# FFN weight signs moved to the head of attention, one store awaited later, a fill split over two engines, bias loads moved: a conv + attention + FFN kernel on one Trainium2 core

## Chip, cores and metric

One core of one Trainium2 chip runs the whole program. The metric is the device time of one execution in microseconds (us). The kernel before takes 2920.16 us, the median of 3 runs (2918.62 to 2920.73).

## What is computed

The input `x` is 32 images of 96 channels and 32 x 32 positions. Three residual stages follow each other:

```python
x = x + _L0_conv_ref(_gn(x), ...)          # per image: linear attention over 1024 positions, plus an MLP
t = _to_tokens(x)                          # (32, 1024, 96)
t = t + _L1_attn_ref(_ln_t(t), ...)        # 6 heads of 16, causal softmax attention, 192 (image, head) pairs
t = t + _L1_ffn_ref(_ln_t(t), W1, b1, W2, b2)
```

The FFN uses weights that are reduced to their signs about a mean, in five groups of output features:

```python
for g in range(NUM_GROUPS):                # 5 groups; rows past 5 * gs stay zero
    wg = W[g * gs:(g + 1) * gs]
    z = wg - wg.mean()
    Wb = Wb.at[g * gs:(g + 1) * gs].set(jnp.sign(z))
y = jnp.einsum('btc,oc->bto', x, Wb) + b   # then quantized group-wise over the batch
```

## The kernel before

The program is four blocks in a row: `prepare`, `conv_block`, `causal_attention`, `project_and_ffn`. Within a block each engine runs its own list of instructions, and they meet through semaphores. At the end of a block all engines meet at a barrier, and none goes on before the last has arrived. SP (SyncE) issues nearly all DMAs, on one queue (q1).

**prepare** (lines 74 to 252). SP issues 16 loads of weights and biases (L138) and waits for them. POOL makes identity and mask matrices. DVE and PE turn and fold the weights; every DVE instruction goes through `link`, which waits for its end before the next. The last piece of DVE is the FFN's signs: two memsets of `w["w1"]` and `w["w2"]` (L218, L219), then for each of 5 groups six instructions (L222 to L227): is-greater and is-less against the group's mean, and their difference, for W1 (76 columns of 96 partitions) and for W2 (57 elements of 128 partitions). The results `w["w1"]` and `w["w2"]` are first read in the FFN block.

**conv_block** (lines 282 to 669). A software pipeline over the 32 images; the last product of an image is a packed tile of query, key and value parts (`cb_packed`, 1.5 MB), which SP stores to the DRAM tensor `qkv_rows` (L383). At its end SP waits for all stores:

```python
for r in range(2):
    sp.wait_ge(x1_stored[r], 16 * (BATCH // 2))
    sp.wait_ge(rows_stored[r], 16 * (BATCH // 2))
```

**causal_attention** (lines 688 to 977). A software pipeline over 192 heads. For each head, SP loads its stack of rows from `qkv_rows` (L764, 256 KB; load i is issued once spread i-1 is made), POOL copies it into V and into `SPREAD` (L803 to L816), SP transposes `SPREAD` by DMA (L769) into `TURNED`, PE multiplies (L853), DVE takes maxima (L965), ACT takes exponentials (L928), PE multiplies with V (L888). Heads 0 to 5 are image 0. Before its first head POOL fills the constant parts: V (L788, L790), the ends of `SPREAD` in all 6 slots (L791), ones (L793, L794). DVE sets two small tiles (L942, L943).

**project_and_ffn** (lines 980 to 1384). Per image: PE turns the attention rows (`turn_att`, L1128), ACT copies them out (`copy_att`, L1214), PE projects them (L1157), DVE adds bias and residual (L1334, with the bias `BP`), then norm, first FFN product with `w["w1"]` (L1111), maxima, and seven rounds later GELU and the second product with `w["w2"]` (L1187). At its head SP issues two loads of attention rows (L1055), eight of x1 quarters (L1060) and eight of bias columns (L1068, L1070, for `BP` and `B2`). ACT and DVE wait for all eight bias loads (`b2_loaded` at 128) before their first work.

## Time and profile before

| what | value |
|---|---|
| median of 3 runs | 2920.16 us |
| the profiled execution | 2919.42 us, its span 2917.7 us |
| PE busy | 2750.0 us (94%) |
| DVE busy | 2300.3 us (79%) |
| ACT busy | 2020.9 us (69%) |
| POOL busy | 1156.5 us (40%) |
| TensorE clock granted, mean | 0.977 |
| DMA | 316.04 MB, mean 108 GB/s |
| block borders in the span | 35.7, 1009.5 and 2438.6 us |

Busy time is the share of the span in which an engine has an instruction under way. The kernel goes through four blocks with barriers between them, so these shares are means over blocks; what happens at a border is seen only in the instructions in order of time.

### The profile page before, as it was taken

What the parts mean: (1) busy time and instruction counts of PE and PEld (TensorE: products, weight loads), DVE (VectorE), ACT (ScalarE), POOL (GpSimd) and SP (SyncE); (2) the same over time, 40 slices, a digit from 0 to 9 for tenths busy, and PEclk for the clock granted to TensorE, in tenths of its full rate; (3) what the DMA queues carried; (4) which work ended last, traced back from release to release, by engine and by line L of the source; (5) the groups of instructions that cost most, each with busy time, mean ns of one, the idle gap of its engine ahead of it and who ended that gap; (6) DMA issues with size and microseconds to landing.
All of it is one profiled execution on the core that took longest, in us unless ns stands there. A gap on an engine that the chain in (4) does not pass through costs nothing. (4 is left out here: it accounts for less than half of the span.)

```text
span 2917.7 us, 86416 instructions
## 1 busy us (share of the span) xinstructions
PE 2750.0 (94%) x29306; PEld 1683.2 (58%) x29306; DVE 2300.3 (79%) x4591; ACT 2020.9 (69%) x3943; POOL 1156.5 (40%) x1999
## 2 busy tenths in 40 slices
PE   3899999999999499999999999999999996899996
PEld 2555555555554266666666666666666664455553
DVE  4576766766666399999999999999999993678997
ACT  1677777777776367777777777777777774577775
POOL 0153434434444444444444444444444431224445
PEclk9999999999999689999999999999999998999998
DMA  1113232332332476666666666666666663334555
GB/s 34 36 63 107 83 113 82 107 110 78 113 113 66 132 127 118 118 117 117 117 117 117 117 117 117 117 117 117 117 117 117 117 114 82 98 99 136 147 139 155
DMA packets 923408, 316.04 MB, mean 108 GB/s; under 512 B 848785, under 2 KB 906418, under 8 KB 923314
## 3 DMA queue, kind: packets, MB, share of 16 engines
q1 hardware_dynamic: 921970, 313.59, 47.6%
q8 instruction: 60, 0.98, 0.1%
q10 hardware_dynamic: 1344, 1.18, 0.1%
q14 instruction: 34, 0.28, 0.0%
HBM read 113.35 MB, written 99.88 MB: 73 GB/s over the span
## 5 line engine op out<-in xcount | busy, mean ns | idle before, releaser
L965 DVE TENSOR_REDUCE at_unit_max<-at_ps_queries 128x1 f32<-128x512 f32 (+4 forms) x2304 | 1135.0, 549 | 89.0 <-PE at_ps_queries L853 86.6
L928 ACT ACTIVATE at_probs<-at_ps_keys 128x512 f32<-128x512 f32 x1344 | 743.3, 603 | 387.6 <-PE at_ps_keys L868 383.0
L853 PE MATMUL at_ps_queries<-at_turned 96*128 96x128 bf16 (+3 forms) x3456 | 634.4, 274 | 33.1 <-DMA at_turned<-at_spread 32.3
L868 PE MATMUL at_ps_keys<-at_turned 128*128 128x128 bf16 (+3 forms) x3456 | 648.7, 275 | 1.8 <-ACT at_probs L928 1.5
L803 POOL TENSOR_TENSOR at_v<-at_stacks,at_one 128x128 f32<-128x128 f32 x192 | 76.9, 401 | 813.0 <-DMA at_stacks<-qkv_rows 813.0
L888 PE MATMUL at_ps_values<-at_probs,at_v 128*32 128x128 f32 x10752 | 373.4, 276 | 6.5 <-ACT at_probs L928 6.4
L868 PEld LDWEIGHTS at_ps_keys<-at_turned 128*128 128x128 bf16 x3456 | 237.8, 97 | 239.5 <-ACT at_probs L928 88.6
L853 PEld LDWEIGHTS at_ps_queries<-at_turned 96*128 96x128 bf16 x3456 | 289.3, 97 | 124.4 <-DMA at_turned<-at_spread 34.0
L888 PEld LDWEIGHTS at_ps_values<-at_probs,at_v 128*32 128x32 f32 x10752 | 269.5, 109 | 120.5 <-ACT at_diag_probs L928 70.2
L928 ACT ACTIVATE at_diag_probs<-at_ps_keys 128x512 f32<-128x512 f32 x384 | 208.6, 595 | 8.2 <-PE at_ps_keys L868 5.3
L822 POOL TENSOR_SCALAR_AFFINE_SELECT at_diag_probs<-at_diag_probs 128x1024 f32<-128x1024 f32 x192 | 210.6, 1097 | 0.0
L580 PE MATMUL cb_ps_hidden<-cb_xn_t,fc 96*128 96x512 f32 x384 | 184.8, 611 | 8.4 <-ACT cb_hidden_t L561 8.4
L491 POOL TENSOR_TENSOR cb_o_hat<-cb_o,cb_o_scale 128x768 f32<-128x768 f32 x32 | 48.1, 1503 | 357.2 <-DVE cb_o_scale L407 357.2
L641 PE MATMUL cb_ps_out<-cb_hidden_t,fc 128*96 128x512 f32 x384 | 175.9, 594 | 0.0
L1111 PE MATMUL ff_ps_hidden<-ff_xn_t,w 97*128 97x512 f32 x360 | 171.0, 609 | 1.8 <-ACT ff_xn_t L1228 1.8
L1202 ACT ACTIVATE ff_hidden<-ff_ps_hidden 128x512 f32<-128x512 f32 x180 | 104.6, 597 | 94.4 <-PE ff_ps_hidden L1111 94.4
L561 ACT ACTIVATE cb_hidden_t<-cb_ps_hidden,fc_bias 128x512 f32<-128x512 f32 x192 | 128.5, 686 | 57.9 <-PE cb_ps_hidden L580 57.5
L471 DVE SCALAR_TENSOR_TENSOR cb_o<-cb_q_norm_v,cb_ps_hidden 128x768 f32<-128x768 f32 x32 | 30.5, 954 | 166.6 <-PE cb_ps_hidden L667 166.6
L1265 POOL TENSOR_TENSOR ff_scale<-ff_var_sums,ff_minus_half 128x8 f32<-128x8 f32 x30 | 49.5, 1650 | 252.7 <-DVE ff_var_sums L1352 252.7
L857 PE MATMUL at_ps_queries<-mask_queries,ident_bf 128*128 128x512 bf16 x384 | 147.7, 385 | 0.0
L1306 DVE TENSOR_REDUCE ff_max<-ff_hidden 128x1 f32<-128x1024 f32 x90 | 109.5, 1217 | 37.4 <-ACT ff_hidden L1202 37.4
L580 PEld LDWEIGHTS cb_ps_hidden<-cb_xn_t,fc 96*128 96x128 f32 x384 | 65.7, 192 | 101.0 <-ACT cb_hidden_t L561 71.4
(212 smaller groups left out, 5028.3 us busy)
## 6 DMA issues: line engine op xcount, KB each, us to landing
qkv_rows<-cb_packed SPq DMA_DIRECT2D x32, 1536.0 KB, 8.2
at_stacks<-qkv_rows SPq DMA_DIRECT2D x192, 256.0 KB, 3.3
cb_x<-in_x_dram SPq DMA_DIRECT2D x32, 384.0 KB, 3.7
cb_x_again<-in_x_dram SPq DMA_DIRECT2D x32, 384.0 KB, 4.6
x_after_conv<-cb_x SPq DMA_DIRECT2D x32, 384.0 KB, 5.0
attention_rows<-at_att SPq DMA_DIRECT2D x384, 32.0 KB, 2.2
ff_att_rows<-attention_rows SPq DMA_DIRECT2D x32, 384.0 KB, 4.4
ff_x<-x_after_conv SPq DMA_DIRECT2D x128, 96.0 KB, 2.4
```

The lines of the kernel that those rows point to most:

```text
L561: act.activation(HT[:, r, k, a * BANK:(a + 1) * BANK], pf[:, a * BANK:(a + 1) * BANK], ACT.Silu, bias=w["fc1_bias"][:, k:k + 1]).then_inc( ...
L580: pe.matmul(pf[:, a * BANK:(a + 1) * BANK], w["fc1"][:, k * P:(k + 1) * P], XNT[:, a * BANK:(a + 1) * BANK], start=True, stop=True).then_i ...
L641: pe.matmul(po[0:C, half], w["fc2"][:, k, :], HT[:, q, k, half], start=(k == 0), stop=False)
L822: pool.affine_select(out=blocks, in_=blocks, compare_op=ALU.is_ge, fill=0.0, base=0, pattern=[[0, TILES], [1, P]], channel_multiplier=-1). ...
L853: mm = pe.matmul(pq[:, u % QBANKS, c0:c0 + n], QT[0:STACK, slot, qb * P:(qb + 1) * P], KT[0:STACK, slot, k0:k0 + n], start=(c0 == 0), stop ...
L857: mm = pe.matmul(pq[:, u % QBANKS, :], w["ident_bf"][:, :], w["mask_queries"][:, :], start=False, stop=True, skip_group_check=True)
L868: mm = pe.matmul(pk[:, bank_k, c0:c0 + n * P], KT[:, slot, kb * P:(kb + 1) * P], QT[:, slot, q0 * P:(q0 + n) * P], start=(c0 == 0), stop=True,
L888: mm = pe.matmul(pv[row:row + VW, col:col + P], V[:, slot, kb, :], probs[:, c0:c0 + P], start=(v == 0), stop=True, skip_group_check=True)
L928: act.activation(probs, pk[:, (slot * NU + k) % KBANKS, :], ACT.Exp, scale=scale).then_inc(S["probs"], 1)
L965: dve.tensor_reduce(peaks, scores, AX.X, ALU.max).then_inc(S["unit_max"], 1)
L1111: pe.matmul(pf[:, a * BANK:(a + 1) * BANK], w["w1"][:, k * P:(k + 1) * P], XNT[:, a * BANK:(a + 1) * BANK], start=True, stop=True).then_in ...
L1306: dve.tensor_reduce(G1[:, n // GB % 2, c:c + 1], Y1[:, n % SLOTS1, k, :], AX.X, ALU.max, apply_absolute_value=True).then_inc(S["y1_max"], 1)
```

## The change

1. **Signs.** The 32 DVE instructions that make the FFN's signs leave `prepare`. The transposed weights and the two tiles of group means (`mean1`, `mean2`) become constants that live on, and DVE makes the signs at the head of `causal_attention`, after its memsets: 2 small memsets of the columns past the groups, 20 comparisons, one wait, and 2 subtractions over all groups at once. The intermediate tiles (`A1`, `B1`, `A2`, `B2`) have no reuse between groups, so nothing waits in between.
2. **Store.** `rows_stored` is made outside the blocks. At the end of `conv_block` SP waits for all stores but the last of `rows_stored[1]` (image 31); the wait for that one stands in `causal_attention` before SP's seventh load.
3. **Fill.** POOL fills the ends of slot 0 of `SPREAD` alone, DVE those of slots 1 to 5 in two memsets, at its head. POOL waits for all three before it goes on.
4. **Biases.** `bp` and `b2` are loaded in `prepare`, by 8 DMAs behind the 16 others, with a semaphore that SP alone awaits. The FFN block neither loads them nor waits for them.

```diff
             @block.sync
             def _(sp):
                     for dst, src in loads:
                         sp.dma_start(dst, src).then_inc(loaded, 16)
+                    for dst, src in quarters:
+                        sp.dma_start(dst, src).then_inc(biases, 16)
                 sp.wait_ge(loaded, 16 * NLOADS)
+                sp.wait_ge(biases, 16 * len(quarters))
...
-                link(dve.memset(w["w1"][0:C, :], 0.0))
-                link(dve.memset(w["w2"][:, :, :], 0.0))
-                for g in range(GROUPS):
-                    c1, c2 = slice(g * gs1, (g + 1) * gs1), slice(g * gs2, (g + 1) * gs2)
-                    link(dve.tensor_scalar(z1[:, c1], w1_t[:, c1], m1[:, g:g + 1], None, ALU.is_gt))
-                    link(dve.tensor_scalar(n1[:, c1], w1_t[:, c1], m1[:, g:g + 1], None, ALU.is_lt))
-                    link(dve.tensor_tensor(w["w1"][0:C, c1], z1[:, c1], n1[:, c1], ALU.subtract))
-                    link(dve.tensor_scalar(z2[:, :, c2], w2_t[:, :, c2], m2[:, g:g + 1], None, ALU.is_gt))
-                    link(dve.tensor_scalar(n2[:, :, c2], w2_t[:, :, c2], m2[:, g:g + 1], None, ALU.is_lt))
-                    link(dve.tensor_tensor(w["w2"][:, :, c2], z2[:, :, c2], n2[:, :, c2], ALU.subtract))
...
                 for r in range(2):
                     sp.wait_ge(x1_stored[r], 16 * (BATCH // 2))
-                    sp.wait_ge(rows_stored[r], 16 * (BATCH // 2))
+                sp.wait_ge(rows_stored[0], 16 * (BATCH // 2))
+                sp.wait_ge(rows_stored[1], 16 * (BATCH // 2 - 1))
...
                 def body(i, r, lap, on):
+                    if isinstance(i, int) and i == SLOTS:
+                        sp.wait_ge(rows_stored[1], 16 * (BATCH // 2))
                     if on(0):
                         _above(sp.wait_ge, S["spread"], i)
                         sp.dma_start(ST[:, r, :, :], src[i]).then_inc(loaded[r], 16)
...
-                pool.memset(SPREAD[:, :, :, :, STACK:P], 0.0).then_inc(S["ends_set"], 1)
-                pool.wait_ge(S["ends_set"], 1)
+                pool.memset(SPREAD[:, 0:1, :, :, STACK:P], 0.0).then_inc(S["ends_set"], 1)
+                pool.wait_ge(S["ends_set"], 3)
...
             @block.vector
             def _(dve):
+                dve.memset(SPREAD[:, 1:SLOTS, 0, :, STACK:P], 0.0).then_inc(S["ends_set"], 1)
+                dve.memset(SPREAD[:, 1:SLOTS, 1, :, STACK:P], 0.0).then_inc(S["ends_set"], 1)
                 dve.memset(MX[:, :, :, :], -3.0e38).then_inc(S["max_set"], 1)
                 dve.memset(MP[:, :, :], 0.0).then_inc(S["parts_set"], 1)
                 dve.wait_ge(S["max_set"], 1)
                 dve.wait_ge(S["parts_set"], 1)
+
+                gs1, gs2 = HIDDEN // GROUPS, C // GROUPS
+                dve.memset(w["w1"][0:C, GROUPS * gs1:HIDDEN], 0.0)
+                dve.memset(w["w2"][:, :, GROUPS * gs2:C], 0.0)
+                for g in range(GROUPS):
+                    c1, c2 = slice(g * gs1, (g + 1) * gs1), slice(g * gs2, (g + 1) * gs2)
+                    mean1, mean2 = w["mean1"][:, g:g + 1], w["mean2"][:, g:g + 1]
+                    dve.tensor_scalar(A1[:, c1], w["w1_t"][:, c1], mean1, None, ALU.is_gt)
+                    dve.tensor_scalar(B1[:, c1], w["w1_t"][:, c1], mean1, None, ALU.is_lt)
+                    dve.tensor_scalar(A2[:, :, c2], w["w2_t"][:, :, c2], mean2, None, ALU.is_gt)
+                    dve.tensor_scalar(B2[:, :, c2], w["w2_t"][:, :, c2], mean2, None, ALU.is_lt
+                                      ).then_inc(S["sides"], 1)
+                dve.wait_ge(S["sides"], GROUPS)
+                dve.tensor_tensor(w["w1"][0:C, 0:GROUPS * gs1], A1[:, :], B1[:, :], ALU.subtract)
+                dve.tensor_tensor(w["w2"][:, :, 0:GROUPS * gs2], A2[:, :, :], B2[:, :, :], ALU.subtract)
...
                 load_x1(1)
-                with nc.allow_non_contiguous_dma(reason="bias columns, once"):
-                    for q in range(4):
-                        sp.dma_start(BP[q * QP:(q + 1) * QP, :], bp.rearrange("(b c) -> c b", c=QP)
-                                     ).then_inc(b2_loaded, 16)
-                        sp.dma_start(B2[q * QP:(q + 1) * QP, :], b2.rearrange("(b c) -> c b", c=QP)
-                                     ).then_inc(b2_loaded, 16)
...
             @block.scalar
             def _(act):
-                act.wait_ge(b2_loaded, 128)
-
...
                 dve.wait_ge(S["half_set"], 2)
-                dve.wait_ge(b2_loaded, 128)
```

How the instructions move, at three places. First DVE at the end of the preparation (`w` is the sign tile, `z` and `n` the two comparisons, `m` or `mean` the group means); before:

```order
L215 COPY m<-prep 96x5
L216 COPY m<-prep 128x5
L218 MEMSET w 96x384
L219 MEMSET w 128x288
L222 TENSOR_SCALAR z<-w_t,m 96x76
L223 TENSOR_SCALAR n<-w_t,m 96x76
L224 TENSOR_TENSOR w<-z,n 96x76
L225 TENSOR_SCALAR z<-w_t,m 128x3x19
L226 TENSOR_SCALAR n<-w_t,m 128x3x19
L227 TENSOR_TENSOR w<-z,n 128x3x19
```

and of the change:

```order
L221 COPY fc<-prep 128x288
L222 COPY mean<-prep 96x5
L223 COPY mean<-prep 128x5
L137 UNCONDITIONAL_BRANCH
L387 UNCONDITIONAL_BRANCH
L447 BN_STATS cb_stats<-cb_x 96x6 x2
```

The copy of the second means is now the last thing that DVE does before the border (the branches), and the statistics of the first image follow. Next DVE at the head of attention, of the change (`at_w_above`, `at_w_below` are the comparisons, `at_unit_max` the maxima of the first head):

```order
L942 MEMSET at_spread 128x5x8x16
L943 MEMSET at_spread 128x5x8x16
L944 MEMSET at_unit_max 128x48
L945 MEMSET at_max_parts 128x128
L950 MEMSET w 96x4
L951 MEMSET w 128x3
...
L957 TENSOR_SCALAR at_w_above<-w_t,mean 128x3x19
L958 TENSOR_SCALAR at_w_below<-w_t,mean 128x3x19
L961 TENSOR_TENSOR w<-at_w_above,at_w_below 96x380
L962 TENSOR_TENSOR w<-at_w_above,at_w_below 128x3x95
L982 TENSOR_REDUCE at_unit_max<-at_ps_queries 128x1 x2
```

Before, only the memsets of `at_unit_max` and `at_max_parts` stood ahead of the first maxima; now two fills stand ahead of them, and the sign work behind them. Last, SP at the head of the FFN; before:

```order
L1055 DMA ff_att_rows<-attention_rows 128x8x96 x2
L1060 DMA ff_x<-x_after_conv 32x3x256 x8
L1068 DMA ff_bp<-in_L_attn_bp_dram 32x3x1
L1070 DMA ff_b<-in_L_ffn_b_dram 32x3x1
...
L1055 DMA ff_att_rows<-attention_rows 128x8x96 [waits ff_att_turned]
```

and of the change:

```order
L1071 DMA ff_att_rows<-attention_rows 128x8x96 x2
L1076 DMA ff_x<-x_after_conv 32x3x256 x8
L1071 DMA ff_att_rows<-attention_rows 128x8x96 [waits ff_att_turned]
L1076 DMA ff_x<-x_after_conv 32x3x256 [waits ff_x2_ready]
```

The eight bias DMAs (four pairs) are gone from between the first x1 loads and the third load of attention rows.

## Rows read from the trace of the kernel before

**Rows 1.** Page, costliest groups: the maxima of attention (count, busy, mean ns, idle before).

```profile
L965 DVE TENSOR_REDUCE at_unit_max<-at_ps_queries 128x1 f32<-128x512 f32 (+4 forms) x2304 | 1135.0, 549 | 89.0 <-PE at_ps_queries L853 86.6
```

**Rows 2.** Instructions in order of time, preparation: start us, length us, engine, line, operation.

```profile
7.77 0.43 SPq L138 DMA_DIRECT2D projb<-in_L_conv_proj_b_dram  x1
...
25.63 0.17 DVE L216 COPY m<-prep 128x5 f32<-128x5 f32 x1
...
34.68 0.26 DVE L226 TENSOR_SCALAR n<-w_t,m 128x57 f32<-128x57 f32 x1
34.97 0.22 DVE L227 TENSOR_TENSOR w<-z,n 128x57 f32<-128x57 f32 x1
...
35.66 55.69 SPq L374 DMA_DIRECT2D cb_x<-in_x_dram  x5
```

**Rows 3.** Page, DMA issues: count, KB each, median us from issue to landing.

```profile
at_stacks<-qkv_rows SPq DMA_DIRECT2D x192, 256.0 KB, 3.3
...
ff_b<-in_L_ffn_b_dram SPq DMA_DIRECT2D x4, 0.4 KB, 2.9
```

**Rows 4.** Instructions in order of time, from the end of conv into attention.

```profile
1003.33 0.37 SPq L383 DMA_DIRECT2D qkv_rows<-cb_packed  x1
...
1009.48 0.74 POOL L788 MEMSET at_v<- 128x768 f32 x1 [7.96 <-POOLq L368]
...
1010.35 2.67 POOL L791 MEMSET at_spread<- 128x3072 bf16 x1
...
1013.38 0.40 POOL L803 TENSOR_TENSOR at_v<-at_stacks,at_one 128x128 f32<-128x128 f32 x1
...
1021.11 0.62 DVE L965 TENSOR_REDUCE at_unit_max<-at_ps_queries 128x1 f32<-128x128 f32 x2 [11.33 <-PE at_ps_queries L853]
```

**Rows 5.** Busy time by stretch; the last two columns: DMA share, GB/s.

```profile
1004.00:1005.00 1.00, 0.00 (x0) 0.00 (x0) 0.00 (x0) 0.00 (x0) 0.00 (x0) 0.50 0.72 275
...
1008.00:1009.00 1.00, 0.00 (x0) 0.00 (x0) 0.00 (x0) 0.00 (x0) 0.00 (x0) 0.50 0.52 186
...
1011.00:1012.00 1.00, 0.00 (x0) 0.00 (x0) 0.00 (x0) 0.00 (x0) 1.00 (x1) 0.50 0.79 178
```

**Rows 6.** SP's queue in order of time, late in conv.

```profile
893.76 0.43 SPq L383 DMA_DIRECT2D qkv_rows<-cb_packed  x1
894.24 1.05 SPq L377 DMA_DIRECT2D cb_x_again<-in_x_dram  x1
```

**Rows 7.** Line 377, the loads `cb_x_again`: from issue to landing.

```profile
DMA to landing us min/median/max: 4.1/4.6/10.0
```

**Rows 8.** Instructions in order of time, head of the FFN.

```profile
2439.66 4.09 SPq L1060 DMA_DIRECT2D ff_x<-x_after_conv  x8
...
2442.07 1.91 PE L1128 MATMUL ff_ps_turn<-ident,ff_att_rows 128*96 128x128 f32 x8 [7.12 <-DMA ff_att_rows<-attention_rows]
...
2447.10 0.43 SPq L1070 DMA_DIRECT2D ff_b<-in_L_ffn_b_dram  x1
...
2450.24 1.02 ACT L1214 ACTIVATE ff_att_t<-ff_ps_turn 96x1024 f32<-96x1024 f32 x1 [15.79 <-DMA ff_b<-in_L_ffn_b_dram]
...
2451.32 2.79 PE L1157 MATMUL ff_ps_out<-ff_att_t,wp 96*32 96x256 f32 x24 [7.34 <-ACT ff_att_t L1214]
...
2454.36 1.27 DVE L1334 SCALAR_TENSOR_TENSOR ff_x<-ff_ps_out,ff_bp,ff_x 128x256 f32<-128x256 f32 x3 [14.35 <-PE ff_ps_out L1157]
```

**Rows 9.** In order of time, end of conv: one POOL operation twice, and DVE.

```profile
980.59 1.60 POOL L498 TENSOR_TENSOR cb_packed<-cb_a_qkv,cb_a_scale 128x768 f32<-128x768 f32 x1 [7.46 <-DMA qkv_rows<-cb_packed]
...
990.53 1.76 DVE L425 TENSOR_TENSOR cb_a_qk<-cb_a_qkv,cb_a_scale 128x1536 f32<-128x1536 f32 x1
990.58 3.04 POOL L498 TENSOR_TENSOR cb_packed<-cb_a_qkv,cb_a_scale 128x768 f32<-128x768 f32 x1 [0.50 <-DVE cb_a_scale L422]
```

**Rows 10.** Busy time by stretch, head of the FFN; the seventh figure is the granted clock.

```profile
2452.00:2456.00 4.00, 4.00 (x30) 2.38 (x23) 1.27 (x3) 0.00 (x0) 0.00 (x0) 0.50 0.00 0
```

**Rows 11.** The chain that ended last: its longest piece in one FFN round.

```profile
2560.20 4.02 PE ff_ps_out L1187 x72
```

More of the change, by code:

```diff
@@ L70, in _constants @@
     w["eps"] = sb("eps", [P, 1])
+    w["bp"] = sb("bp", [P, 3])
+    w["b2"] = sb("b2", [P, 3])
+    w["w1_t"] = sb("w1_t", [C, HIDDEN])
+    w["w2_t"] = sb("w2_t", [P, CHUNKS, C])
+    w["mean1"] = sb("mean1", [C, GROUPS])
+    w["mean2"] = sb("mean2", [P, GROUPS])
     return w
@@ L89, in prepare @@
         w1_raw = sb("w1_raw", [P, CHUNKS, C])
[L90 removed]
+        w1_t = w["w1_t"]
         w2_raw = sb("w2_raw", [C, HIDDEN])
[L92 removed]
+        w2_t = w["w2_t"]
         lng = sb("lng", [C, 1])
@@ L111, in prepare @@
         products, step = sem("prep_products"), sem("prep_step")
+        biases = sem("prep_biases")
         gs1, gs2 = HIDDEN // GROUPS, C // GROUPS
@@ L131, in prepare @@
         NLOADS = len(loads)
+        quarters = [(w[name][q * C // 3:(q + 1) * C // 3, :], A[src].rearrange("(b c) -> c b", c=C // 3))
+                    for name, src in (("bp", "L1_attn_bp"), ("b2", "L1_ffn_b2")) for q in range(4)]
         MADE = 14
@@ L279, in _dmas, with conv_block @@
     return (lap + ((slot - back) // slots + 1)) * 16
-def conv_block(nc, w, x_in, x1, rows):
+def conv_block(nc, w, x_in, x1, rows, rows_stored):
     with ExitStack() as ctx:
@@ L356, in conv_block @@
         x1_stored = [sem(f"x1_stored{i}") for i in range(2)]
-        rows_stored = [sem(f"rows_stored{i}") for i in range(2)]
         names = ("bn_parts bn_done mv_ready g_done g_copied gn_var gn_std gn_scale xs_ready qkv_psum qkv_copied "
@@ L685, in _quarter, with causal_attention @@
     return qb if qb < half else TILES - 1 - qb
-def causal_attention(nc, w, rows, att):
+def causal_attention(nc, w, rows, rows_stored, att):
     scale = C ** -0.5
@@ L730, in causal_attention @@
         QT = TURNED[:, :, 1, :, :].rearrange("p s t n -> p s (t n)")
+        A1, B1 = (sb(f"w1_{side}", [C, GROUPS * (HIDDEN // GROUPS)]) for side in ("above", "below"))
+        A2, B2 = (sb(f"w2_{side}", [P, CHUNKS, GROUPS * (C // GROUPS)]) for side in ("above", "below"))
         MX = sb("unit_max", [P, 2, TILES, 3])
@@ L1386, in build @@
         prepare(nc, w, A)
-        conv_block(nc, w, x_in, x1, rows)
-        causal_attention(nc, w, rows, att)
-        project_and_ffn(nc, w, att, x1, x2, y_out, A["L1_attn_bp"], A["L1_ffn_b2"])
+        rows_stored = [ctx.enter_context(nc.semaphore(f"rows_stored{i}")) for i in range(2)]
+        conv_block(nc, w, x_in, x1, rows, rows_stored)
+        causal_attention(nc, w, rows, rows_stored, att)
+        project_and_ffn(nc, w, att, x1, x2, y_out)
 _INS = ['x', 'L0_conv_qkv_w', 'L0_conv_proj_w', 'L0_conv_proj_b', 'L0_conv_ln_g', 'L0_conv_ln_b',
```

16 lines of the change are left out of this document (4 added, 12 removed).

## The prediction

> **What bounds the kernel now.** The page's shares are means over four blocks, so I read them only for the pace inside a block. In attention, nearly half of the span, DVE takes maxima almost without a break [rows 1]: 2304 of them, 1135.0 us busy against 89.0 us idle. Nothing in the change touches that loop, nor the loops of conv and FFN. What it touches are the three borders between blocks, where all engines stand at a barrier and every us is on the path. So I read the borders in the timeline, each for two things: which engine arrives last, and which wait ends last behind it.
>
> First border: the last instruction before it is a DVE one, the last of the signs, ending at 34.97 + 0.22 = 35.19, and conv's first load is issued at 35.66 [rows 2]. So DVE arrives last, and the barrier costs 0.47 us.
>
> Second border: SP issues the last row store at 1003.33, done with issuing at 1003.70, and POOL starts attention at 1009.48 [rows 4]. In between only the store moves: the DMA engines run at 275 GB/s and more until half of the slice from 1008 [rows 5]. So the wait for the landing comes last. Behind the border POOL fills until 1013.38, 2.67 us of it `SPREAD`, then starts the first head [rows 4].
>
> Third border: PE turns the first attention rows by 2442.07 + 1.91 = 2443.98, yet ACT copies them only at 2450.24, released by a bias load whose issue was at 2447.10 [rows 8]. PE's projection and DVE's sum come behind ACT.
>
> **Part 1, signs out of the preparation: -9.4 us.** DVE's last work becomes the copy that ends at 25.63 + 0.17 = 25.80 [rows 2]. With the same 0.47 us, conv starts at 26.27 in place of 35.66: 9.39 us. What could be late next is SP, which now issues 8 more loads: from 8.20 on, 8 x 0.47 us (0.43 and a gap) brings it to 12.0 [rows 2], and such a load lands 2.9 us after issue [rows 3], so at 14.9, 10.9 us before DVE is done. They stand behind the 16 others in the queue, so DVE's first wait does not see them. Cost nothing, while DVE has that work.
>
> **Part 2, the signs at the head of attention: nothing on the path.** DVE there waits for PE until 1021.11 [rows 4]. What now stands before that: two fills of 5 slots, together at most 2.67 x 5/6 = 2.2 us at POOL's rate; four small memsets, at most 0.26 each, 1.0; 20 comparisons of 0.26, 5.2; two subtractions, each at most five of the old ones (0.22), 2.2 [rows 2, 4]. That is 10.6 us at most. With attention starting at 1004.2 (below) DVE is free by 1014.8; the first maxima are due at 1021.11 less the 3.2 us of part 3, 1017.9. Cover: 3.1 us; were it gone, each us more would be a us.
>
> **Part 3, the store awaited later, and the fill: -3.2 us.** SP arrives at 1003.70, so attention starts at about 1004.2 with the barrier's 0.5: 5.3 us earlier. But POOL's first head needs stack load 0, and that is issued on the queue on which the store is still moving. What it takes is not shown for this place, so I bound it.
> - If it runs free: 3.3 us after issue [rows 3], 1007.5. POOL's own fills are shorter now (slot 0 alone, 0.45 in place of 2.67) and wait for DVE's 2.2 us at most, so they are done by about 1006.7. Start at 1007.5, gain 5.9.
> - If it pays its whole 3.3 us after the store has landed at about 1009.0: 1012.3, gain 1.1.
> - If its bytes simply follow the store's: the store's end at 1008.5, the load's take 1.15 us (a slice of 0.79 share holds most of them), landing 0.5 after its last byte as the store's does [rows 5]: 1010.15, gain 13.38 - 10.15 = 3.23.
>
> I take the third. Late in conv a load is issued 0.5 us behind a row store [rows 6]. The line of such loads has a median of 4.6 us from issue to landing and a maximum of 10.0 [rows 7]: 5.4 us more, a little over the 4.3 us for which the store's bytes move at the border [rows 5]. The Trainium skill, "DMA: Bandwidth & Descriptors", section "Queues, rings and completion order", says that an engine takes descriptors in ring order and that a semaphore's increment lands only behind all earlier writes of that engine. By that the gain of 5.9 could not be had; the maximum agrees [rows 7]. So the split of the fill earns nothing by itself: the load (1010.15) is later than even the old fills would be (1004.2 + 3.9 = 1008.1). The wait moved to SP's seventh load is long over when SP comes to it. The seven POOL instructions of head 0, the DMA turn and PE follow at their old distances, and so does every head behind them, as DVE sets their pace.
>
> **Part 4, biases: -6.2 us.** ACT's first copy starts when PE's turn is done, 2444.0 in place of 2450.24: 6.24 us [rows 8]. DVE's sum moves from 2454.36 to 2448.1. It needs the x1 loads, issued by 2439.66 + 4.09 = 2443.75; even with the 3.3 us of a larger load they are in at 2447.1 [rows 3, 8]. The third load of attention rows is issued 3.5 us earlier as well, directly behind x1. So the whole 6.24 us goes on.
>
> **Sum.** 9.39 + 3.23 + 6.24 = 18.9 us. Against the profiled execution, 2919.42 - 18.9 = 2900.5; the median of the runs is 0.7 above that execution, so 2901.3. What the sum leaves out is the clock: at the FFN's head PE runs at a granted 0.50, that is 1.2 GHz [rows 10], after its idle time at the border, and where it rises again relative to the work may shift. A projection of an image takes 2.79 us at that level [rows 8]; at 2.4 GHz it would be half. One such image more or less is 1.4 us, at each of three block heads: some 2.5 us either way.
>
> **Rivals.**
> 1. *DVE's signs hold POOL up.* The same POOL operation takes 1.60 us when it starts first, and 3.04 when a DVE operation with two SBUF inputs has started 0.05 us ahead [rows 9]. If comparisons do this too and the signs last beyond 1010.15, each of the 7 instructions of head 0 waits for one of 0.26 us: 1.8 us back, 2903.1. For it: at the upper bound DVE works until 1014.8. Against: the bound is generous, and back to back DVE should be done near 1011. [...]
> 2. *The load starts its own cost after the store:* gain 1.1 in part 3, 2903.4.
> 3. *The load overtakes the store:* gain 5.9, 2898.6. The maximum of 10.0 us is against it [rows 7].
> 4. *The border does not let go:* the barrier's end waits for SP's outstanding transfer anyway, so part 3's wait is not removed. Then only the fill counts: the load lands at 1009.48 + 3.3 = 1012.8, gain 0.6, sum 16.2, 2904.0. Nothing in the timeline shows such a wait.
> 5. *Eaten elsewhere:* 13 us or more of the gain come back through longer half-clock stretches at the block heads, say 15 us: 2916. It needs ten images more at 1.4 us; one or two are plausible.
> 6. *Slower:* the earlier FFN start puts whole rounds at 1.2 GHz. The second product has 4.02 us of PE in a round [rows 11]; at half clock it is 8.0. From the seventh such round on (7 x 4.02 = 28.1 us) the gain is more than lost; with ten, 40.2 - 18.9 = 21.3, so 2941.5. Against it: PE has hardly a pause in those rounds, and their work does not change.
>
> **How the numbers follow.** Chances: forecast 0.70, rival 1 0.08, rival 2 0.06, rival 3 0.05, rival 4 0.05, rival 5 0.04, rival 6 0.02. A measurement of this kernel tells 0.2%, 5.8 us, from no change. All but rivals 5 and 6 are faster than that: 0.94; same 0.04; slower 0.02. The range takes the forecast with the clock's 2.5 us (2898.8 to 2903.8), rivals 1, 2 and 4, and some of the clock's spread on top of them: 2897 to 2906.
>
> **What would show it.** Conv's first load at 26.3. Then all conv at its old distances, the last row store at 994, attention's first POOL memset 0.5 us behind the end of its issue, V of head 0 about 6.8 us behind it, DVE idle again before the first maxima. At the FFN, ACT's first copy directly behind PE's turn, 5.4 us after the border. I am wrong in part 3 if V of head 0 starts 3.3 us after its load's issue, or over 8; wrong in part 2 if the first maximum finds its matmul done; wrong on the clock if the blocks' inner lengths change by over 3 us.

## The result, and the profile after

| | us | runs |
|---|---|---|
| before, on the same chip | 2920.44 (2918.62 to 2921.72) | 4 |
| after | 2901.82 (2899.99 to 2903.19) | 4 |
| ratio | 0.9936, 95% interval 0.9919 to 0.9954 | |
| profiled execution of after | 2903.19, its span 2901.5 | 1 |

The change makes the kernel 18.6 us (0.64%) faster. The forecast was 2901.3 us, in a range from 2897 to 2906. The profiled execution of after is the highest of its four, so the two profiled spans (2917.7 and 2901.5) differ by 16.2 us only. The medians are the result; the traces say where each us is. The interval of the ratio allows 13 to 24 us, so the time alone does not tell the forecast from rivals 1 to 4 (2898.6 to 2904.0); where V of head 0 starts does.

From the page of after: the busy times of the engines, and the line of the maxima that answers to [rows 1] (count, busy, mean ns, idle before).

```profile
PE 2730.6 (94%) x28924; PEld 1685.7 (58%) x29306; DVE 2300.3 (79%) x4585; ACT 2020.8 (70%) x3943; POOL 1153.0 (40%) x1999
...
L982 DVE TENSOR_REDUCE at_unit_max<-at_ps_queries 128x1 f32<-128x512 f32 (+4 forms) x2304 | 1135.9, 550 | 86.0 <-PE at_ps_queries L853 83.5
```

DVE is busy for 2300.3 us as before, and the maxima have not moved. The page cannot show this change: it lies at the three borders.

**First border** (against [rows 2]), in order of time: start, length, engine, line, operation.

```profile
10.12 1.84 SPq L144 DMA_DIRECT2D b<-in_L_ffn_b_dram  x4
...
25.64 0.17 DVE L223 COPY mean<-prep 128x5 f32<-128x5 f32 x1
...
26.30 0.80 SPq L369 DMA_DIRECT2D cb_x<-in_x_dram  x2
...
29.85 1.28 DVE L447 BATCH_NORM_STATS2 cb_stats<-cb_x 96x6 f32<-96x512 f32 x2 [4.05 <-DMA cb_x<-in_x_dram]
```

DVE's last work ends at 25.81 and conv's first load is issued at 26.30, in place of 35.66: 9.36 us. SP issued the last bias load by 11.96 and did not delay anything. The last line shows the next wait: DVE idles 4.05 us, the border's 0.5 included, for the first image.

**Second border** (against [rows 4]), the same view.

```profile
994.21 0.37 SPq L378 DMA_DIRECT2D qkv_rows<-cb_packed  x1
995.19 0.74 POOL L788 MEMSET at_v<- 128x768 f32 x1 [2.80 <-POOLq L363]
995.19 8.77 SPq L764 DMA_DIRECT2D at_stacks<-qkv_rows  x2
...
996.06 0.59 DVE L943 MEMSET at_spread<- 128x640 uint32 x1
...
997.02 0.26 DVE L955 TENSOR_SCALAR at_w_above<-w_t,mean 96x76 f32<-96x76 f32 x1
...
1000.90 0.44 DVE L962 TENSOR_TENSOR w<-at_w_above,at_w_below 128x285 f32<-128x285 f32 x1
1001.75 0.40 POOL L803 TENSOR_TENSOR at_v<-at_stacks,at_one 128x128 f32<-128x128 f32 x1 [4.83 <-DMA at_stacks<-qkv_rows]
...
1009.00 0.64 DVE L982 TENSOR_REDUCE at_unit_max<-at_ps_queries 128x1 f32<-128x128 f32 x2 [7.66 <-PE at_ps_queries L853]
```

Attention starts 0.98 us after the store's issue (6.15 before). POOL, done with its fills, waits 4.83 us for the stack of head 0. V of head 0 starts 7.54 us after the store's issue, 10.05 before: 2.5 us gained. DVE ends the signs at 1001.34 and waits 7.66 us for the first matmul.

**Third border** (against [rows 8]).

```profile
2428.12 0.11 POOL L1263 MEMSET ff_minus_half<- 128x8 f32 x1 [9.81 <-POOLq L756]
...
2431.74 1.91 PE L1138 MATMUL ff_ps_turn<-ident,ff_att_rows 128*96 128x128 f32 x8 [7.25 <-DMA ff_att_rows<-attention_rows]
...
2433.68 1.02 ACT L1222 ACTIVATE ff_att_t<-ff_ps_turn 96x1024 f32<-96x1024 f32 x1 [9.68 <-PE ff_ps_turn L1138]
...
2437.68 1.27 DVE L1341 SCALAR_TENSOR_TENSOR ff_x<-ff_ps_out,bp,ff_x 128x256 f32<-128x256 f32 x3 [8.12 <-PE ff_ps_out L1167]
```

ACT's copy starts 0.03 us after PE's turn, 5.56 us behind the border (POOL's first line), against 11.66 before: 6.10 us. DVE's sum is released by PE, not by the x1 loads.

**Inside the blocks.** From conv's first load to the last row store it is 967.9 us (967.7 before), from V of head 12 to V of head 191 1305.7 in both, from ACT's first copy in the FFN to the end 467.8 (467.5). One place is longer: from V of head 0 to V of head 12, 80.0 us against 78.9. DVE's last step of the maxima of the second, third and fourth head, of before:

```profile
1033.44 0.18 DVE L969 TENSOR_REDUCE at_neg_max<-at_unit_max 128x8 f32<-128x24 f32 x1
...
1040.17 0.18 DVE L969 TENSOR_REDUCE at_neg_max<-at_unit_max 128x8 f32<-128x24 f32 x1
...
1047.71 0.18 DVE L969 TENSOR_REDUCE at_neg_max<-at_unit_max 128x8 f32<-128x24 f32 x1
```

and of after, the second and third (the fourth is at 1037.21):

```profile
1021.43 0.18 DVE L986 TENSOR_REDUCE at_neg_max<-at_unit_max 128x8 f32<-128x24 f32 x1
...
1029.27 0.18 DVE L986 TENSOR_REDUCE at_neg_max<-at_unit_max 128x8 f32<-128x24 f32 x1
```

The third head takes 7.84 us in place of 6.73 and the fourth 7.94 in place of 7.54; later ones take 7.2 in both. The windows show that the clock rises later there (busy time of PE, PEld, DVE, ACT, POOL, then granted clock, DMA share, GB/s; each window begins with V of head 0). Before:

```profile
1013.38:1037.00 23.62, 15.14 (x62) 6.42 (x63) 15.07 (x36) 3.03 (x6) 9.67 (x37) 0.50 0.69 134
```

After:

```profile
1001.75:1028.20 26.45, 17.73 (x72) 8.02 (x75) 17.72 (x41) 4.68 (x8) 10.23 (x37) 0.50 0.68 134
```

Both stretches are granted 0.50 (1.2 GHz) throughout and are followed by one at full speed. That of after lasts 2.8 us longer: it ends 6.8 us into the third head (counted from 1021.43), against 3.6 before (from 1033.44). Whether the longer heads come from that is asked below.

Summed over the profiled executions: 9.36 + 2.5 + 6.10 = 18.0 gained at the borders, 1.1 lost in the first heads, 0.2 in conv and 0.3 in the FFN's own length, and rounding: 16.2.

### The profile page after: what moved, and what is told of

Its sections match the earlier page's. It is cut to its first block and busy times, and to the rows that moved or that the text cites. A ratio compares the mean times of both kernels' runs of the same rounds, so it can differ in the third digit from the quotient of the medians.

```text
span 2901.5 us, 86028 instructions
## 1 busy us (share of the span) xinstructions
PE 2730.6 (94%) x28924; PEld 1685.7 (58%) x29306; DVE 2300.3 (79%) x4585; ACT 2020.8 (70%) x3943; POOL 1153.0 (40%) x1999
## 5 line engine op out<-in xcount | busy, mean ns | idle before, releaser
L868 PE MATMUL at_ps_keys<-at_turned 128*128 128x128 bf16 x3453 | 648.4, 275 | 13.3 <-ACT at_probs L928 1.7
L637 PEld LDWEIGHTS cb_ps_out<-cb_hidden_t,fc 128*96 128x96 f32 x384 | 62.9, 164 | 102.0 <-issue 102.0
```

The source lines that it names most:

```text
L637: pe.matmul(po[0:C, half], w["fc2"][:, k, :], HT[:, q, k, half], start=(k == 0), stop=False)
L868: mm = pe.matmul(pk[:, bank_k, c0:c0 + n * P], KT[:, slot, kb * P:(kb + 1) * P], QT[:, slot, q0 * P:(q0 + n) * P], start=(c0 == 0), stop=True,
```

## The experiments

The theory: the three gains are independent and of the sizes read above; the signs at attention's head cost nothing because they lie beside waits; the stack load's bytes follow the store's. The rivals: DVE's comparisons hold POOL up, the load pays in full behind the store, a gain is eaten elsewhere. The first four experiments each undo one part of the change. They ran on one chip (before there: 2919.19 us, 2917.99 to 2926.39, 13 runs). All diffs are against after. A median is compared with after's in two ways, straight, and by how far each lies below before on its own chip (18.6 us for after); where the two differ, both are given.

**Signs back in the preparation.**

```diff
+                link(dve.memset(w["w1"][0:C, :], 0.0))
...
+                    link(dve.tensor_scalar(z1[:, c1], w1_t[:, c1], m1[:, g:g + 1], None, ALU.is_gt))
...
-                dve.tensor_tensor(w["w2"][:, :, 0:GROUPS * gs2], A2[:, :, :], B2[:, :, :], ALU.subtract)
```

> The changed kernel, but with the signs made in the preparation as before, and nothing of them at the head of attention. Theory (9.4 us of DVE work left the path and cost nothing where it went): conv's first load at 35.7 us in place of 26.3, all else as changed, so about 9.4 us slower than the changed kernel, 2911 us. Rival (the signs at the head of attention hold POOL or the first maxima up): less than 9.4 us slower, since that loss goes away: V of head 0 would start less than 6.5 us behind the block border.

Measured: 2910.64 us (2908.01 to 2916.59, 9 runs), ratio 0.997 [0.996, 0.998]. Conv starts at 35.69. V of head 0 starts 7.54 us after the store's issue, as with the signs beside it, and the third head takes 7.5 us. The run is 8.8 to 10.1 us above after. So the signs are worth their 9.4 us in the preparation and cost nothing in attention, and the longer third head does not come from them.

**The store awaited in conv again.**

```diff
-                sp.wait_ge(rows_stored[1], 16 * (BATCH // 2 - 1))
+                sp.wait_ge(rows_stored[1], 16 * (BATCH // 2))
```

> The changed kernel, but SP waits for the last row store at the end of conv, as before. Theory (the first stack load's bytes queue behind the store's, and the barrier is open meanwhile): the border comes 6.2 us after the last store's issue, the load is alone and lands about 3.0 us after its issue, POOL's short fills (1.7 us) are done by then, so V of head 0 starts about 9.2 us after the store's issue, against 7.5 in the changed kernel and 10.05 before: 1.7 us slower than the changed kernel, 2903.5. Rival (the load pays its whole cost after the store anyway): no difference, V at 9.0 or later in both.

Measured: 2903.68 us (2901.29 to 2904.96), ratio 0.9941 [0.9928, 0.9955]. In order of time:

```profile
995.46 0.37 SPq L378 DMA_DIRECT2D qkv_rows<-cb_packed  x1
...
1001.60 0.39 SPq L762 DMA_DIRECT2D at_stacks<-qkv_rows  x1
...
1003.24 0.10 POOL L792 MEMSET at_one<- 128x1 f32 x1
1004.59 0.40 POOL L801 TENSOR_TENSOR at_v<-at_stacks,at_one 128x128 f32<-128x128 f32 x1 [1.26 <-DMA at_stacks<-qkv_rows]
```

A stack load on an empty queue is usable 2.99 us after its issue. V starts 9.13 us behind the store's issue, between 10.05 before and 7.54 after: the fill alone brings 0.9 (POOL is free at 1003.34, and the load is now the later one), the late wait 1.6 more. The medians put the late wait at 1.9 to 3.1 us.

**The biases loaded in the FFN again.**

```diff
-                    for dst, src in quarters:
-                        sp.dma_start(dst, src).then_inc(biases, 16)
...
+                        sp.dma_start(B2[q * QP:(q + 1) * QP, :], b2.rearrange("(b c) -> c b", c=QP)
+                                     ).then_inc(b2_loaded, 16)
...
+                act.wait_ge(b2_loaded, 128)
...
+                dve.wait_ge(b2_loaded, 128)
```

> The changed kernel, but with the eight bias loads at the head of the FFN and the waits for them. Theory: ACT's first copy 11.6 us after the border in place of 5.6, so 6 us slower than the changed kernel, 2908. Rival (the earlier start is partly eaten by the clock or by the x1 loads): less than 5 us slower.

Measured: 2907.64 us (2906.15 to 2910.94), ratio 0.9958 [0.9945, 0.9972]. ACT's row of before is back:

```profile
2438.96 1.02 ACT L1228 ACTIVATE ff_att_t<-ff_ps_turn 96x1024 f32<-96x1024 f32 x1 [16.25 <-DMA b<-in_L_ffn_b_dram]
```

It starts 12.12 us behind the border (5.56 in after), and the time is 5.8 to 7.1 us above after's.

**POOL fills all six slots again.**

```diff
-                pool.memset(SPREAD[:, 0:1, :, :, STACK:P], 0.0).then_inc(S["ends_set"], 1)
-                pool.wait_ge(S["ends_set"], 3)
+                pool.memset(SPREAD[:, :, :, :, STACK:P], 0.0).then_inc(S["ends_set"], 1)
+                pool.wait_ge(S["ends_set"], 1)
...
-                dve.memset(SPREAD[:, 1:SLOTS, 0, :, STACK:P], 0.0).then_inc(S["ends_set"], 1)
-                dve.memset(SPREAD[:, 1:SLOTS, 1, :, STACK:P], 0.0).then_inc(S["ends_set"], 1)
```

> The changed kernel, but POOL fills all six slots alone, 2.7 us. Theory (stack load 0 ends last): POOL is ready about 4 us after the border, the load lands at 6.5, so V of head 0 starts at the same distance of 6.5 us and the time is the same, 2902. Rival (the split is what made part 3's gain): up to 2.2 us slower, V of head 0 later by that.

Measured: 2902.79 us (2902.12 to 2903.14), ratio 0.994 [0.9926, 0.9953].

```profile
995.41 2.84 DVE L955 TENSOR_SCALAR at_w_above<-w_t,mean 128x57 f32<-128x57 f32 x1
995.46 2.76 POOL L791 MEMSET at_spread<- 128x3072 bf16 x1
...
998.42 0.13 POOL L794 MEMSET at_one<- 128x1 f32 x1
...
1000.68 0.55 DVE L959 TENSOR_TENSOR w<-at_w_above,at_w_below 96x380 f32<-96x380 f32 x1
1001.15 0.71 POOL L803 TENSOR_TENSOR at_v<-at_stacks,at_one 128x128 f32<-128x128 f32 x1 [2.59 <-DMA at_stacks<-qkv_rows]
```

POOL is free at 998.55 and still waits 2.59 us; V starts 6.56 us behind the border, the figure of after to 0.01. So the split brings V's start nothing beside the late wait, and 0.9 us without it (the run with the store awaited in conv). The median is 1.0 to 2.2 us above after's, but the profiled span is not (2901.1 against 2901.5) and the intervals of the two ratios overlap: a small worth of the split in time is left open.

The rows also bear on rival 1. DVE's comparisons beside POOL's fill of 2.76 us last 2.84 (the one shown), 2.70 and 2.58 us, where 0.25 is usual. And V, which starts while DVE's first subtraction (two inputs in SBUF) is under way, lasts 0.71 us in place of 0.40: here DVE does hold POOL up, by 0.3 us.

The next four ran beside one another (before 2919.98 us, 2918.19 to 2921.44, 9 runs).

**The wait for the store moved ahead of the first stack load.** Attention still starts early, but the load does not queue behind the store.

```diff
-                    if isinstance(i, int) and i == SLOTS:
+                    if isinstance(i, int) and i == 0:
```

> The changed kernel, but SP waits for the last row store before its first stack load, inside attention; the barrier, the fills and the signs are not held up. Theory (the load's reads begin while the store is ending, and slow its last packets): the store's bytes move for 4.3 us, as before, and not for 4.8; it lands 5.6 us after issue; the load then pays 3.3 us, so V of head 0 starts about 9.0 us after the store's issue against 7.5: 1.5 us slower, 2903.3. Rival (the longer store is chance, or comes from POOL's and DVE's fills beside it): its bytes move for 4.8 us here too.

Measured: 2903.28 us (2902.47 to 2905.0), ratio 0.9943 [0.9928, 0.9958]. V starts 8.72 us behind the store's issue, against 7.54: to queue the load early wins 1.2 us (1.5 to 1.9 by the medians). What that costs the store is in the windows from 4 us behind the store's issue. This run (store issued at 994.10):

```profile
998.00:999.00 1.00, 0.00 (x0) 0.00 (x0) 1.00 (x7) 0.00 (x0) 0.00 (x0) 0.50 1.03 370
999.00:1000.00 1.00, 0.00 (x0) 0.00 (x0) 1.00 (x7) 0.00 (x0) 0.00 (x0) 0.50 0.26 92
```

After (store issued at 994.21):

```profile
998.00:999.00 1.00, 0.00 (x0) 0.00 (x0) 1.00 (x7) 0.00 (x0) 0.00 (x0) 0.50 1.01 293
999.00:1000.00 1.00, 0.00 (x0) 0.00 (x0) 1.00 (x8) 0.00 (x0) 0.00 (x0) 0.50 0.95 258
```

Alone, the store runs at 370 GB/s in its last full us. With the load queued, the engines are as full but move 293 GB/s. The trace also records every DMA packet. By these records the store's bytes move for 4.37 to 4.38 us in the six of this document's fourteen profiles (before, after and twelve experiments) in which no load follows it that closely, and for 4.95 to 4.97 us in the eight in which the first stack load is issued 0.98 us behind the store. In after the store's packets take 67 to 69 ns at first (median) and 112 to 116 ns from 4.5 to 5.5 us behind the issue. The last of them ends at 5.88 us; the first packet of the load starts at 5.70 and its last ends at 6.79. So the queued load slows the store's end by 0.6 us, and its own bytes follow nearly behind it. How a load whose packets are not yet recorded slows the store is open.

**Four times the comparisons.** 60 more comparisons of the same sizes, into tiles that nothing reads; the outputs do not depend on them.

```diff
+                    for E1, F1, E2, F2 in MORE:
+                        dve.tensor_scalar(E1[:, c1], w["w1_t"][:, c1], mean1, None, ALU.is_gt)
+                        dve.tensor_scalar(F1[:, c1], w["w1_t"][:, c1], mean1, None, ALU.is_lt)
+                        dve.tensor_scalar(E2[:, :, c2], w["w2_t"][:, :, c2], mean2, None, ALU.is_gt)
+                        dve.tensor_scalar(F2[:, :, c2], w["w2_t"][:, :, c2], mean2, None, ALU.is_lt)
```

> The changed kernel with three further sets of the 20 comparisons at the head of attention, into tiles that nothing reads: 60 more DVE instructions of 0.17 us, about 10 us. Theory (comparisons do not block POOL; the cover ahead of the first maxima is 7.7 us): POOL's seven instructions of head 0 take 1.8 us as before though DVE works beside them, DVE ends about 2.4 us after the first maxima were due, and the kernel is 2 to 2.5 us slower, 2904. Rival (each comparison locks POOL out of SBUF): the seven take up to 3.6 us, and the first head is later by up to 1.8 us more.

Measured: 2902.33 us (2901.66 to 2905.52), ratio 0.9943 [0.9927, 0.9958]. Here the comparisons do run beside POOL's first head:

```profile
1000.23 0.43 POOL L805 TENSOR_TENSOR at_v<-at_stacks,at_one 128x128 f32<-128x128 f32 x1 [4.82 <-DMA at_stacks<-qkv_rows]
1000.27 0.43 DVE L963 TENSOR_SCALAR at_w_below<-w_t,mean 96x76 f32<-96x76 f32 x1
1000.61 0.34 POOL L809 COPY at_spread<-at_stacks 128x192 uint32<-128x192 uint32 x1
1000.63 0.36 DVE L964 TENSOR_SCALAR at_w_above<-w_t,mean 128x57 f32<-128x57 f32 x1
...
1001.84 0.23 POOL L818 COPY at_spread<-at_stacks 128x64 uint32<-128x64 uint32 x1
...
1010.84 1.81 DVE L989 TENSOR_REDUCE at_unit_max<-at_ps_queries 128x1 f32<-128x128 f32 x4
```

POOL's seven instructions take 1.84 us, against 1.81 in after. It is DVE that waits: a comparison that starts beside a POOL instruction lasts as long as that one (0.43, 0.36; alone 0.25). So for comparisons rival 1's mechanism is the wrong way round. And the cover in part 2 is real: DVE is busy until the first maxima, which start 10.61 us behind V of head 0 in place of 7.25, and from V of head 0 to V of head 12 it is 83.0 us in place of 80.0. The median shows 0.5 to 1.0 us of this, less than the 2 to 2.5 expected. In the profiled execution the rest is hidden by a shorter FFN (below) and a conv 1.5 us shorter; whether that holds for all four runs is open.

**Stack 0 loaded into a tile of its own, before the border.** Its rows belong to image 0, stored long ago; the load waits only until 15 of the 16 stores of the even images are in.

```diff
+                    if isinstance(i, int) and i == BATCH + 6:
+                        sp.wait_ge(rows_stored[0], 16 * (BATCH // 2 - 1))
...
+                        sp.dma_start(w["stack0"][:, :, :], first).then_inc(loaded0, 16)
```

> The changed kernel, but stack load 0 goes into a tile of its own and is issued in conv, just ahead of the last row store. Theory (the load behind the store bounds the border): V of head 0 starts when POOL's fills are done, 1.7 us behind the border in place of 6.6, load 1 still comes in time behind the store: 4.9 us faster than the changed kernel, 2897. Rival (the next load, behind the store, or the clock takes it back): less than 2.5 us faster.

Measured: 2895.27 us (2894.68 to 2895.92), ratio 0.9915 [0.9902, 0.9929].

```profile
993.65 0.74 POOL L795 MEMSET at_v<- 128x768 f32 x1 [2.80 <-POOLq L364]
...
995.47 0.40 POOL L811 TENSOR_TENSOR at_v<-stack,at_one 128x128 f32<-128x128 f32 x1
...
1000.75 0.40 POOL L811 TENSOR_TENSOR at_v<-at_stacks,at_one 128x128 f32<-128x128 f32 x1 [3.46 <-DMA at_stacks<-qkv_rows]
```

V of head 0 follows POOL's fills directly, 1.82 us behind the border in place of 6.56. The 4.7 us go on to the heads behind, although head 1 still waits for its load: DVE's maxima of head 0 cover that. The medians show 6.1 to 6.6 us. The profile is 8.1 us shorter than after's; what is more than 4.7 lies in the blocks' own lengths (conv 966.4 us against 967.9, the heads 0.9 less, the FFN 466.8 against 467.8). So in after the stack load is what the head of attention waits for.

**The FFN's first loads issued at the end of attention.** Attention rows and x1 of images 0 and 1, by SP behind its last loads, into tiles that outlive the block.

```diff
+                    if isinstance(i, int) and i == NHEADS + 3:
+                        for q in range(SLOTS):
+                            sp.wait_ge(stored[q], 2 * 16 * (NHEADS // SLOTS - 2))
...
+                            sp.dma_start(AR[:, n, :, :], att[n].rearrange("(t p) c -> p t c", p=P)
+                                         ).then_inc(a_loaded[n], 16)
...
-                load_att(0)
-                load_att(1)
-                load_x1(0)
-                load_x1(1)
```

> The changed kernel, but the FFN's first two loads of attention rows and eight of x1 are issued by SP near the end of attention, after its heads 0 to 179 are stored. Theory (after the change the FFN's head is bound by these loads): PE turns the first rows 0.2 us behind the border in place of 3.6, 3.4 us faster, 2898.4. Rival (the 0.8 MB delay the last attention stores, or PE's clock starts lower for it): less than 1.7 us faster.

Measured: 2898.38 us (2897.22 to 2900.63), ratio 0.9928 [0.9915, 0.9942].

```profile
2427.88 0.10 POOL L1268 MEMSET ff_minus_half<- 128x8 f32 x1 [9.84 <-POOLq L756]
...
2429.37 1.94 PE L1143 MATMUL ff_ps_turn<-ident,ff_att_rows 128*96 128x128 f32 x8 [5.15 <-DVE ff_xn_t L1291]
...
2431.34 1.02 ACT L1227 ACTIVATE ff_att_t<-ff_ps_turn 96x1024 f32<-96x1024 f32 x1 [7.62 <-PE ff_ps_turn L1143]
```

ACT's copy starts 3.46 us behind the border (5.56 in after). The time agrees with the forecast (3.0 to 3.4 us faster), the mechanism only in part: 2.1 us come from the loads, and PE now waits for a row of ones that DVE writes at its head. In the profile the remainder is in the FFN's own length, 464.9 us against 467.8, of which more below.

The next three (before 2919.45 us, 2917.12 to 2921.53, 9 runs) ask about the clock, and join the two last gains.

**PE kept at work at the head of attention.** 160 matmuls of the identity with itself, into a bank that is written over later; the outputs do not depend on them.

```diff
+                for _ in range(160):
+                    pe.matmul(bank[:, 3 * P:4 * P], w["ident_bf"][:, :], w["ident_bf"][:, :], start=True, stop=True)
```

> The changed kernel with 160 matmuls more at the head of attention, 128 columns each, into an unused part of PSUM, run while PE would wait for the first head. Theory (the third and fourth head are slow when the granted clock rises late, 26.4 us behind V of head 0 in the changed kernel's profile against 23.6 before): the clock is up before the first scores, the third head takes 6.7 us or less in place of 7.8 and the fourth 7.3 in place of 7.9, 1.5 us faster than the changed kernel, 2900.3. Rival (their length comes from the transfers or from DVE): same lengths, no gain, or a loss if the 160 last beyond the first scores.

Measured: 2900.86 us (2898.55 to 2902.23), ratio 0.9935 [0.9922, 0.9949]. Its windows:

```profile
996.00:1002.00 6.00, 5.41 (x52) 5.44 (x53) 5.01 (x27) 0.00 (x0) 1.57 (x5) 0.50 0.95 294
1002.50:1012.80 10.30, 7.93 (x119) 6.70 (x116) 2.29 (x6) 0.00 (x0) 3.60 (x14) 1.00 0.57 113
1013.00:1026.50 13.50, 12.20 (x51) 5.23 (x52) 13.01 (x33) 3.33 (x6) 5.06 (x20) 0.50 0.91 148
```

The clock rises at 1002.5, falls at 1012.8, 4.3 us after the added work has ended (at 1008.5) and beside the first scores, and rises again at 1026.4, 23.2 us behind V of head 0 where after has 26.4. The third head takes 6.8 us (7.8) and V of head 12 comes 78.2 us behind that of head 0 (80.0). This run alone would not prove the cause, for the last rise comes at 23.0 us in two runs whose head of attention is after's (biases undone, FFN loads early), and there too the third head is short, 6.7 us. But over all fourteen profiles third and fourth head together grow with the time at which the clock rises: 13.9 to 14.4 us when it rises 2.9 to 3.9 us into the third head, 14.6 to 15.0 at 4.1 to 5.2, and 15.3 to 15.9 at 6.0 or later. So the longer heads follow the clock, not the signs or the loads, and the 1.1 us that after's profile loses there is no cost of the change. No gain in time is shown: the median is 1.0 us below after's, but against before on its own chip this run is 18.6 us faster, just as after is.

**PE kept at work at the FFN's head.** 45 such matmuls at the end of attention and 30 at the start of the FFN.

```diff
+                for _ in range(45):
+                    pe.matmul(pk[:, 0, 0:P], w["ident_bf"][:, :], w["ident_bf"][:, :], start=True, stop=True)
...
+                for _ in range(30):
+                    pe.matmul(pf[:, 0:P], w["ident_bf"][:, :], w["ident_bf"][:, :], start=True, stop=True)
```

> The changed kernel with 45 such matmuls behind PE's last work in attention and 30 at the head of the FFN, where PE would be idle. Theory (PE starts the FFN at 1.2 GHz for want of work): the first turn takes 1.1 us in place of 1.9, the first projection 1.5 in place of 2.8, the second turn 1.1 in place of 1.9, so about 3 us faster than the changed kernel, 2899. Rival (the FFN's head is paced by the other engines and loads): under 1 us faster.

Measured: 2901.75 us (2900.93 to 2902.97), ratio 0.994 [0.9926, 0.9953]: a miss.

```profile
2430.38 1.05 PE L1142 MATMUL ff_ps_turn<-ident,ff_att_rows 128*96 128x128 f32 x8 [1.88 <-DMA ff_att_rows<-attention_rows]
...
2432.54 2.79 PE L1171 MATMUL ff_ps_out<-ff_att_t,wp 96*32 96x256 f32 x24 [1.11 <-ACT ff_att_t L1226]
```

The turn runs at full clock, 1.05 us in place of 1.91, but the grant falls to 0.50 from 2432.5 to 2439.3, and the projection takes the same 2.79 as in [rows 8]. At the FFN's head the half clock lasts 6.8 us in place of 13.7, yet by the clock records the FFN runs 40.4 us in all at half clock behind ACT's first copy, against 37.7 in after. The half clock was put off, not taken away.

**Stack 0 and the FFN's loads both early**, with PE's wait for the row of ones put behind its first turn.

```diff
-                pe.wait_ge(S["ones_set"], 2)
...
+                    if r == 0:
+                        pe.wait_ge(S["ones_set"], 2)
```

> The changed kernel with stack load 0 ahead of the last row store and the FFN's first ten loads in the end of attention, and PE's wait for DVE's ones moved behind its first turn (with the loads early alone this wait took their place, and ACT's first copy came 3.5 us behind the border in place of 5.6). Theory (the two gains stand at different borders and add; the ones were the next wait): V of head 0 1.8 us and ACT's first copy 2.1 us behind their borders, 4.8 + 3.5 = 8.3 us faster than the changed kernel, 2893.5. Rival (one gain is lost to the other): above 2896.

Measured: 2893.4 us (2891.44 to 2893.72), ratio 0.9911 [0.9896, 0.9926]. V starts 1.82 and ACT's copy 1.99 us behind their borders: 4.7 + 3.6 = 8.3 us, against 7.4 to 8.4 in the medians. The gains add up.

**The first images loaded in the preparation as well** (before 2918.85 us, 2918.25 to 2920.49, 7 runs).

```diff
+                for n in range(2):
+                    sp.dma_start(X[:, n, :], A["x"].rearrange("b c h w -> b c (h w)")[n]).then_inc(x_loaded[n], 16)
...
-                    if on(-1):
+                    if on(-1) and not (isinstance(i, int) and i < 1):
```

> The kernel with both sets of loads early, and conv's first two loads of x also issued in the preparation, behind the biases; the tile for x lives from there on. Theory (each block's head waits for its own first load, and conv's is the last such wait left): DVE's first statistics start 0.1 us behind the first border in place of 3.6, 3.5 us faster than with both early (2893.4): 2890. Rival (conv's head is then bound by ACT's table load or PE's low clock, and the gain goes there): less than 1.5 us, 2892 or above.

Measured: 2889.64 us (2888.28 to 2893.16), ratio 0.9897 [0.9881, 0.9914].

```profile
25.66 0.17 DVE L226 COPY mean<-prep 128x5 f32<-128x5 f32 x1
...
26.35 1.28 DVE L453 BATCH_NORM_STATS2 cb_stats<-cb_x 96x6 f32<-96x512 f32 x2 [0.53 <-PEq L138]
```

DVE's first statistics start 0.52 us after its last copy, 3.50 us earlier than in after; by the medians the step from the run before is 3.2 to 3.8 us. This version beats both kernels: it is 29.2 us below before on the same chip, and 10.6 to 12.2 below after.

**The FFN's length, over all fourteen profiles.** From ACT's first copy to the end it is 464.4 to 464.9 us in three of them (signs undone, four times the comparisons, FFN loads early) and 466.8 to 468.1 in the others. The windows that begin with that copy differ in the clock. After:

```profile
2433.68:2533.68 100.00, 83.00 (x489) 47.08 (x490) 59.78 (x84) 47.65 (x69) 24.88 (x16) 0.89 0.41 116
```

Four times the comparisons:

```profile
2435.52:2535.52 100.00, 81.74 (x517) 45.31 (x517) 61.46 (x87) 50.81 (x72) 24.88 (x16) 0.93 0.41 115
```

In the same 100 us the second gets through 517 recorded matmuls and 87 DVE instructions, the first through 489 and 84. These two kernels have the same FFN, so the 3 us are no cost of the change under test. They are the clock's: the clock records show 30.9 to 31.4 us at half clock between that copy and the end in the three short ones and 36.7 to 40.4 in the others, and the length less half of that time is 447.9 to 449.2 us in all fourteen. Why the grant falls more often in some executions was not found. Conv varies as much, from 966.1 to 969.3 us between its first load and the last row store.

## Why the prediction was right

- **Signs out of the preparation**, forecast 9.39: 9.36 in the trace; undoing it costs 8.8 to 10.1 in the medians. Right, the barrier's 0.5 us included.
- **Signs in attention**, forecast nothing: right, with more cover than thought (7.66 us against 3.1). The bound of 10.6 us of DVE work was generous: it takes 6.2 us from the border, since the two fills take 0.59 us each, in place of 2.2 together, and comparisons follow one another every 0.17 us although each is 0.25 long. The experiment with four times the comparisons shows what happens when the cover is gone.
- **Store and fill**, forecast 3.23: 2.5, the only term off. V comes 7.54 us behind the store's issue, not 6.82. The step that failed is the end of the store in "its bytes simply follow the store's": the load's bytes do follow, from 0.18 us before the store's last, but the store's end is at 5.88 us and not at the 5.17 read from [rows 5]. Of these 0.7 us, 0.6 are what the queued load costs the store (4.97 us in place of 4.38 for its bytes), a cost that the prediction put at nothing. The load's last byte comes 0.91 us behind the store's (1.15 in the sum) and V 0.75 us behind that (0.5), which cancels. Neither end of the bounds held: the load is not free (a gain of 5.9), and it does not pay its whole price behind the store (that is 8.72 us, in the run with the wait moved). The Trainium skill, "DMA: Bandwidth & Descriptors", section "Queues, rings and completion order", says beside its ring order that a later descriptor may finish its write before an earlier one. Packets of both transfers are recorded in the same 0.18 us, but the records do not tell the DMA engines apart, so no run here shows that. That the split of the fill does not move V's start beside the late wait was forecast and is shown (6.56 us behind the border in both).
- **Biases**, forecast 6.24: 6.10 in the trace, 5.8 to 7.1 in the medians. Right.
- **The clock**, left out with 2.5 us either way: the first heads lost 1.1 us in the profiled execution, and over the fourteen profiles that loss follows the time at which the clock rises. The FFN's two lengths, 3 us apart, are of the same size as that allowance.
- **The rivals.** 1 (DVE's signs hold POOL up) did not arise: the signs end at 1001.34, 0.4 us before V starts. With four times the comparisons beside POOL it is DVE that waits; only a subtraction held POOL up, by 0.3 us, in the run in which POOL fills all slots. A price of 1.8 us was seen in no run. The Trainium skill, "SBUF — State Buffer", section "SBUF: two separate sides", says that whichever instruction starts first has the shared port pair for the whole instruction; the stretched comparisons (0.43 beside a POOL instruction of 0.43, 2.84 beside one of 2.76) agree, and POOL's 1.84 us show that a short one ahead of POOL costs it next to nothing. 2 (load after the store) and 3 (load overtakes) fell by V's start. 4 (the border holds on) fell: POOL starts 0.98 us behind the store's issue. 5 and 6 would have shown in the blocks' lengths, which moved by 1.1 us at most in the profile of after.
- The sum of 18.9 stands against 18.6 in the medians and 16.2 in the spans. That the median agrees so closely is in part luck, since 0.7 us of the store and some of the clock were missed, and conv and the FFN each vary by 3 us or more from one execution to another.

## What to carry to other kernels

At a border between blocks two questions find nearly everything: which engine arrives last, and which wait ends last behind it. Short work can leave the end of one block for the head of the next, where its engine waits anyway, but its cover there is the time until that engine's first real work, and it is best tested by adding more of the same work. A load that the next block needs first belongs ahead of the border, in a buffer of its own: here that was worth 3.5 to 4.7 us at each of three borders.

## What the hardware showed that was not expected

- A load queued 0.98 us behind a store on the same queue slows the store's end: 4.38 us for the store's bytes alone and 4.97 with it, its packets 112 to 116 ns in place of 67 to 69 near the end. The load still comes 1.2 us sooner than one issued once the store is awaited.
- Beside POOL instructions it is DVE's comparisons that grow (0.25 us alone, 0.43 beside a POOL instruction of 0.43, 2.84 beside a fill of 2.76), hardly POOL's instructions (1.84 against 1.81 us for seven). A subtraction with two inputs in SBUF that had started first took POOL's next instruction from 0.40 to 0.71 us. Before the change, a DVE operation with two SBUF inputs that had started first took a POOL one from 1.60 to 3.04 us [rows 9].
- 160 added matmuls brought the clock up 0.7 us before V of head 0 in place of 26.4 us behind it, and it fell again for 13.6 us beside real work (PE busy for 12.2 of 13.5 us); 75 at the FFN's head bought one turn (1.05 for 1.91 us) and no time.
- The same FFN took 464.4 to 468.1 us over fourteen profiled executions, with 30.9 to 40.4 us of it at half clock; the length less half of that time stays within 1.3 us. A part worth 3 us can hide in such a spread, so single parts were read from border to border, and only sums from medians.
